# Turning the combine weights of an expert layer by DMA transposes instead of TensorE transposes

## The reference, cut to what matters

```
logits   = einsum('bsd,etd->bset', xn, se)          # 4 batches, 2048 rows, 8 x 128 slots
dispatch = softmax(logits, axis=1)                  # over the rows
slots    = einsum('bsd,bset->betd', xn, dispatch)
h        = gelu(slots @ w1);  processed = h @ w2
combine  = softmax(logits.reshape(b, s, e * t), axis=-1)
out      = x + einsum('bnd,bsn->bsd', processed, combine)
```

## Time and profile before

| what | us |
|---|---|
| median of 3 runs | 1343.07 (1338.6 to 1345.66) |
| the profiled execution, its own time | 1331.78 |
| span of the profiled execution | 1329.8 |
| PE busy | 1187.9 (89%) |
| DVE busy | 924.9 (70%) |
| ACT busy | 745.6 (56%) |
| POOL busy, all of it in `attention` and its set-up | 242.3 (18%) |
| mean granted clock of TensorE, as a share of full speed | 0.946 |

### The profile page before, as it was taken

One profiled execution on the slowest core, in us unless ns is written; L12 is line 12 of the kernel. 1 busy time (PEld: TensorE's weight loads), 2 busy tenths in 40 slices (PEclk: granted clock), 3 DMA queues, 4 the chain that ended last, 5 costly groups with the idle time before them and its releaser, 6 DMA issues.

```text
span 1329.8 us, 27115 instructions
## 1 busy us (share of the span) xinstructions
PE 1187.9 (89%) x8600; PEld 910.9 (68%) x8600; DVE 924.9 (70%) x2130; ACT 745.6 (56%) x1382; POOL 242.3 (18%) x275
## 2 busy tenths in 40 slices
PE   4498888989899885499999999999999999999999
PEld 2377777777777775248779548689558689467688
DVE  4688888887878863399545699445798445898444
ACT  3345565555555424258665558565468665577654
POOL 3555445554444431000000000000000000000000
PEclk8799999888988868699999999999999999999999
DMA  5122222323222121402112103212011212000012
GB/s 170 34 66 77 69 64 76 88 69 87 64 64 64 49 57 60 119 20 64 51 31 75 37 0 64 62 31 79 21 30 35 72 36 74 18 0 1 1 48 71
DMA packets 121979, 73.10 MB, mean 55 GB/s; under 512 B 49984, under 2 KB 119616, under 8 KB 121920
## 3 DMA queue, kind: packets, MB, share of 16 engines
q1 hardware_dynamic: 113200, 64.40, 17.2%
q10 hardware_dynamic: 8656, 7.87, 2.0%
q0 software_dynamic: 64, 0.00, 0.0%
HBM read 38.16 MB, written 25.69 MB: 48 GB/s over the span
## 4 chain that ended last, share of the span: by engine, by line
PE 39%; DVE 9%; issue 7%; ACT 2%; DVEq 1%; ACTq 0%; POOL 0%; POOLq 0%
PE m_wide L1792 13%; PE m_wide L1683 7%; PE m_wide L1770 6%; PE m_wide L1756 6%; PE m_wide L1781 4%; DVE m_Dm L1414 3%; ACT m_Eh L1571 2%; DVE m_cmax L1399 2%; DVE m_rmax L1401 2%; PE m_wide L1730 2%; DVE m_El L1422 1%; PE m_wide L1740 1%; DVE m_mcol L1407 0%; DVE m_sl L1436 0%; ACT m_L L1552 0%
## 5 line engine op out<-in xcount | busy, mean ns | idle before, releaser
L1683 PE MATMUL m_wide<-seT,XT 128*128 128x512 f16 x768 | 169.8, 382 | 30.5 <-ACTq L1543 25.5
L1730 PE MATMUL m_wide<-m_X,m_Eh 128*128 (+1 forms) x1024 | 172.6, 274 | 16.4 <-DVE m_El L1422 16.4
L1683 PEld LDWEIGHTS m_wide<-seT,XT 128*128 (+1 forms) x768 | 75.3, 98 | 121.1 <-ACTq L1543 25.9
L1792 PE MATMUL m_wide<-m_Ph,m_Th 128*128 128x257 f16 x512 | 140.4, 274 | 1.7 <-DVE m_Pl L1453 1.7
L1730 PE MATMUL m_wide<-m_X,m_El 128*128 128x257 f16 (+1 forms) x512 | 139.7, 273 | 0.0
L1792 PE MATMUL m_wide<-m_Ph,m_Tl 128*128 128x257 f16 x512 | 139.4, 272 | 0.0
L1792 PE MATMUL m_wide<-m_Pl,m_Th 128*128 128x257 f16 x512 | 139.1, 272 | 0.0
L1515 DVE TENSOR_TENSOR m_Tl<-m_wide,m_Th 128x1024 f16<-128x1024 f32 x64 | 78.4, 1224 | 68.2 <-ACT m_Th L1610 67.6
L1730 PEld LDWEIGHTS m_wide<-m_X,m_Eh 128*128 128x128 f16 x1024 | 97.7, 98 | 40.3 <-DVE m_El L1422 21.4
L1610 ACT CAST m_Th<-m_wide 128x1024 f16<-128x1024 f32 x64 | 64.7, 1011 | 86.3 <-PE m_wide L1781 86.3
L1564 ACT ACTIVATE m_E<-m_Dm,m_eshift 128x512 f32<-128x512 f32 x128 | 92.0, 722 | 32.0 <-DVE m_Dm L1414 30.7
(11 more groups left out here) (186 smaller groups left out, 2677.0 us busy)
## 6 DMA issues: line engine op xcount, KB each, us to landing
Mrep<-M_dram SPq DMA_DIRECT2D x16, 512.0 KB
x_dram<-x SPq DMA_DIRECT2D x16, 512.0 KB, 2.9
m_X<-X_dram SPq DMA_DIRECT2D x128, 64.0 KB, 1.8
m_x1t<-x_dram SPq DMA_DIRECT2D x64, 128.0 KB, 2.1
out_dram<-m_o SPq DMA_DIRECT2D x64, 128.0 KB, 1.7
x_<-in_L_attn_x_dram ACTq DMA_DIRECT2D x14, 512.0 KB, 4.0
X_dram<-Xh SPq DMA_DIRECT2D x16, 256.0 KB, 2.3
X_dram<-Xl SPq DMA_DIRECT2D x16, 256.0 KB, 5.8
```

The lines of the kernel that those rows point to most:

```text
L1683: last = pe.matmul(lg[t % 4], XT[:, sx * KD + k, bass.ds((4 * g + t) * P, P)], seT[:, ss, k, z * HS:(z + 1) * HS], start=(c == 0), stop=(c ...
L1730: last = pe.matmul(acc[v][q], e[t % 4][:, qs], X[:, sx, bass.ds(4 * g + t, 1), 0:XW].rearrange("q a n -> q (a n)"), start=first and e is E ...
L1792: last = pe.matmul(co[p], a[p][:, es], pp[:, e, 0:XW], start=(c == 0), stop=(c == 3 * NS - 1))
```

## The change

Both halves of the weights are made before they are turned. ACT takes the exponent in place in `L`, waits for it, and copies it to f16 (`Wh`); DVE subtracts (`Wl = L - Wh`). SP turns both by `dma_start_transpose` from SBUF into `Th` and `Tl`, which now have four buffers each and no longer come through PSUM. `Wh` and `Wl` have four buffers too, laid over `Eh`, `El` and `E`: tiles 0 and 1 over `Eh` and `El`, tiles 2 and 3 over `E`. Since `dispatch` reads `Eh` and `El`, ACT waits for both `B_ps` (the last dispatch matmuls) ahead of `weights(0, 0)`; since `hidden` keeps its f32 values in `E`, it waits for `hl_ok` ahead of `weights(0, 2)`. The transposes on TensorE and the tile `Ec` are gone. The loads of `x1t` and the stores of `o` leave SP; POOL issues them, in the same order.

```diff
-                def turn(h, p):
-
-                    n = b * HB + h + 1
-                    pe.wait_ge(Ec_ok[p], n)
-                    pe.wait_ge(Tl_ok[p], n)
-                    for e in range(NS):
-                        last = pe.transpose(tp[p][:, e * P:(e + 1) * P], Ec[p][:, e * P:(e + 1) * P], ident[:, :])
-                    last.then_inc(tp_ps[p], 1)
...
+            def turn(b, k, t):
...
+                sp.wait_ge(co_ps[t % 2], n)
+                sp.sem_inc(turning, 1)
+                sp.wait_ge(Wh_ok[t], m)
+                sp.sem_inc(turning, 1)
+                sp.dma_start_transpose(Th[t][:, :, :], Wh[t]).then_inc(T_in[t], 16)
+                sp.wait_ge(Wl_ok[t], m)
+                sp.sem_inc(turning, 1)
+                sp.dma_start_transpose(Tl[t][:, :, :], Wl[t]).then_inc(T_in[t], 16)
...
+            with pool.Fori(0, B) as b:
+                with pool.Fori(0, HB) as h:
+                    n = pool.snap(b * HB + h + 1)
+                    for p in range(2):
+                        pool.wait_ge(o_ok[p], n)
+                        pool.sem_inc(going, 1)
+                        pool.dma_start(x1t[p][:, :], x1_dram[bass.ds(b, 1), bass.ds(h * 2 * P + p * P, P), :]
+                                       .rearrange("b q d -> (b q) d")).then_inc(x1_in[p], 16)
+                    for p in range(2):
+                        pool.wait_ge(o_ok[p], n + 1)
+                        pool.sem_inc(going, 1)
+                        pool.dma_start(out[bass.ds(b, 1), bass.ds(h * 2 * P + p * P, P), :]
+                                       .rearrange("b q d -> (b q) d"), o[p][:, :]).then_inc(o_out[p], 16)
...
-                    dve.tensor_tensor(Tl[p][:, :], tp[p][:, :], Th[p][:, :], ALU.subtract).then_inc(Tl_ok[p], 1)
...
+                    dve.tensor_tensor(Wl[t], L[:, bass.ds(4 * k + t, 1), :].rearrange("q a n -> q (a n)"), Wh[t],
+                                      ALU.subtract).then_inc(Wl_ok[t], 1)
...
+                    row = L[:, bass.ds(4 * k + t, 1), :].rearrange("q a n -> q (a n)")
+                    act.activation(row, row, ACT.Exp, bias=nrm[:, bass.ds(4 * k + t, 1)]).then_inc(Ec_ok[t], 1)
+                    free = act.snap(act.to_reg(32 * m))
+                    act.wait_ge(pc, 1)
+                    act.wait_ge(Ec_ok[t], m)
+                    act.wait_ge(T_in[t], free)
+                    act.copy(Wh[t], row).then_inc(Wh_ok[t], 1)
...
                 act.wait_ge(A_dve, nb)
+                for p in range(2):
+                    act.wait_ge(B_ps[p], (2 * b + 2) * HB + 2)
                 weights(0, 0)
                 hidden_high(0)
...
+                processed_high(1, range(0, 2))
+                for p in range(2):
+                    act.wait_ge(hl_ok[p], (2 * b + 2) * (NF // 2) + 2)
+                weights(0, 2)
+                processed_high(1, range(2, QS))
+                weights(0, 3)
...
+                def combine(k, t):
+                    p, n = t % 2, b * HB + 2 * k + t // 2 + 1
+                    pe.wait_ge(T_in[t], 32 * (b * QB + k + 2))
                     pe.wait_ge(o_ok[p], n)
```

More of the change, by code:

```diff
@@ L1291, in moe @@
         Pl = sb("Pl", [P, NS, XS], F16)
-        Ec = two("Ec", [P, E_SLOTS])
-        Th = two("Th", [P, E_SLOTS], F16)
-        Tl = two("Tl", [P, E_SLOTS], F16)
+        Th = [sb(f"Th{u}", [P, NS, P], F16) for u in range(4)]
+        Tl = [sb(f"Tl{u}", [P, NS, P], F16) for u in range(4)]
         cden = two("cden", [P, 1])
@@ L1327, in _ @@
         def _(sp):
-            for p in range(2):
-                sp.sem_inc(o_out[p], 16)
+            for u in range(4):
+                sp.sem_inc(T_in[u], 32)
             def load_XT(b):
@@ L1343, in load_X, with turns @@
                                      .rearrange("b q d -> (b q) d")).then_inc(X_in, 16)
[L1345 to L1355, removed]
+            def turn(b, k, t):
+                m = sp.snap(sp.to_reg(b * QB + k + 1))
+                n = sp.snap(sp.to_reg(b * HB + 2 * k + t // 2 + 1))
+                sp.wait_ge(pc, 1)
+                sp.wait_ge(co_ps[t % 2], n)
[6 more added lines that the diff above has]
+                sp.dma_start_transpose(Tl[t][:, :, :], Wl[t]).then_inc(T_in[t], 16)
+            def turns(b):
+                with sp.Fori(0, QB) as k:
+                    for t in range(4):
+                        turn(b, k, t)
             sp.sem_inc(XT_in, 32)
@@ L1448, in hidden_low, with processed_low @@
                             .then_inc(hl_ok[f % 2], 1)
-                def processed_low(v):
-                    for q in range(QS):
+                def processed_low(v, qs):
+                    for q in qs:
                         dve.wait_ge(Ph_ok[q % 2], (2 * b + v) * (QS // 2) + q // 2 + 1)
@@ L1526, in finish @@
                                              ALU.mult, ALU.add).then_inc(o_ok[p], 1)
+                slots_low(0)
+                slots_out(1, range(QS))
                 low_weights(0, 0)
-                processed_low(1)
+                hidden_low(0)
+                slots_low(1)
+                processed_low(0, range(QS))
+                hidden_low(1)
                 low_weights(0, 1)
[L1531 to L1536, removed]
+                processed_low(1, range(0, 2))
+                low_weights(0, 2)
+                processed_low(1, range(2, QS))
+                low_weights(0, 3)
+                with dve.Fori(0, QB - 1) as k:
+                    for t in range(4):
+                        finish(k, t)
+                        low_weights(k + 1, t)
+                for t in range(4):
+                    finish(QB - 1, t)
         @block.scalar
@@ L1831, in _ @@
                     pe.wait_ge(Pl_ok[p], cut_to)
-                with pe.Fori(0, HB - 1) as h:
-                    for p in range(2):
-                        combine(h, p)
-                        turn(h + 1, p)
-                for p in range(2):
-                    combine(HB - 1, p)
+                with pe.Fori(0, QB) as k:
+                    for t in range(4):
+                        combine(k, t)
 def build(nc, io, out):
```

87 lines of the change are left out of this document (37 added, 50 removed).

## The result

The changed kernel takes 1374.64 us (median of 4 runs, 1366.12 to 1381.67), beside 1340.84 us for the kernel before (4 runs, 1336.38 to 1345.66). The ratio is 1.0249 with a 95% interval of 1.0178 to 1.0320: it is slower by 2.5%. All ratios here are taken from fast executions alone, since now and then an execution of any kernel is 1 to 2% longer at a lower granted clock (two of the four of e3 are, its profiled one among them). The profiled execution took 1373.25 us, with a span of 1371.7.

A forecast was written before the change was run, and what follows sets the result against it. TensorE was taken to bound the kernel before, the residual loop on POOL the changed one. Four batches at -1.5 us are -6, the end adds +2: 1343 - 4 = 1339 us, with a range of 1312 to 1385.

The forecast's parts named there:

- c: Residual loop in the combine stage: time from one odd finish's end to the next's, forecast 6.95 us for two tiles.
- GpSimd instead of SyncE: Residual loop: two longer issues on POOL add 0.4 to 0.8 us, taken as 0.6; no extra landing time.
- the transposes in the way: Residual loop: a 256 KB transpose ahead holds the DMA engines 0 to 0.9 us; half, 0.45, was taken.
- The end of the stage: End of each batch's combine stage: last two combines need 3.2 us after the loops, ending at 741.9 us in batch 0.
- The lead-in: Ahead of the combine stage: PE waits 1.7 us a batch in hidden(0); with processed(1), the stage starts 2.35 us later.
- SP's loop: SP issuing two transposes a tile in the combine stage: 3.2 us a tile, ending at 738.2, ahead of 741.9.
- T: SP's time to issue one 128 x 1024 transpose: taken as 1.3 us, deciding the pace from 1.45 on.
- SP as the pace: Rival, combine stage: transposes take 1.70 us to issue, a tile 4.0 us; 1363 us in all, chance 0.17.
- Dear source: Rival, combine stage: transposes out of SBUF cost more than out of DRAM; at 2.5 us each 1443 us, chance 0.09.
- DVE holding POOL: Rival, residual loop: low_weights on DVE holds up POOL's store issue for 1.29 us; c 8.24, 1370 us, chance 0.07.
- POOL as quick as SP: Rival, residual loop: POOL no slower than SP; c 5.9, -7.8 us a batch, 1313 us, chance 0.17.
- The four tiles: Rival, combine stage: a tile's way through four buffers, some 7.4 us, keeps tiles from getting ahead; given nothing.

The follow-up runs named there:

- e3: Changed kernel with only the high half of the weights turned by DMA and used again in place of the low half: ratio 1.0208 to the kernel before.
- e2: Changed kernel with GpSimd issuing each next residual load ahead of the store: 1340.72 us, ratio 1.0052 to the kernel before.
- e5: Changed kernel without any DMA transposes in the combine stage, which reads constant weights: 1337.4 us, ratio 0.9997 to the kernel before.
- e4: Changed kernel with tile 0's copy moved behind hidden(0), only its exp staying ahead: 1367.39 us, ratio 1.0284 to the kernel before.
- e1: Kernel before with residual loads and result stores issued by GpSimd, transposes still on TensorE: 1334.87 us, ratio 1.0021.
- e7: Changed kernel with the load ahead of the store, plus one spare 128 KB load a tile from GpSimd: 1372.62 us, ratio 1.0243 to the kernel before.
- e9: Changed kernel with load ahead of store and tile 0's copy later, odd tiles turned on TensorE again: 1308.81 us, ratio 0.9833 to the kernel before.
- e8: Changed kernel with load ahead of store and tile 0's copy and low half behind hidden(0): 1330.25 us, ratio 0.9965 to the kernel before.
- e6: Changed kernel with load ahead of store and only the high half turned, used again for the low: 1309.61 us, ratio 0.9766 to the kernel before.

## Why the prediction was wrong, point by point

**What bounds the stage: right.** The residual loop replaced TensorE as the pace, as forecast; the waits, the pairs of gaps and the place are those named. e2 shows it by removal. The range given for this very case, 1323 to 1354 (c of 6.3 to 7.6), does not hold the time; the wide one, 1312 to 1385, does only by its rivals.

**The term that failed: c, forecast 6.95 us, measured 8.21**, and with it the sign, since break-even stood at 7.2. By its parts:

| part of c | forecast | measured | from |
|---|---|---|---|
| loop before, with its rest | 5.9 | 5.56 | rest 2.21, not 2.55 |
| GpSimd instead of SyncE | +0.6 | +0.92 | e5 |
| the transposes in the way | +0.45 | +1.73 | changed kernel against e5 |
| sum | 6.95 | 8.21 | |

The third row is the miss: it is 1.28 us off, and the two others, 0.34 too high and 0.32 too low, cancel by luck. The working bounded it by 0 to 0.9 us, the bytes of one transpose at the full rate, and took half. That assumed one transpose in front of the load, at random, and a load that is served at once behind it. In the trace nothing is random: SP's transposes of a pair wait for the `low_weights` behind the even finish, which the load before has released; they come out one behind the other, one mostly 0.8 us ahead of the load and the next mostly 0.5 to 0.8 behind it, in every round but a batch's last. And the price is not that of the bytes. In 22 of these 24 rounds the load lands within 0.25 us of the transpose issued just ahead of it, 3.8 to 4.5 us after its own issue, as if it were served together with the whole of it; why, no run shows. e3, with one transpose issued 0.65 us ahead of the load, still costs 1.38 us (3.75 - 2.37), over the bound. Even at the bound c would have been 7.4 and the time, by the prediction's own sum, 1350: the sign, but not the size.

The second row was a third too low, and priced the wrong thing. The longer issue (0.54 us against 0.36) does not count: store to load is 1.20 us on POOL and 1.27 on SP. What counts is GpSimd's reaction to the semaphore, 0.70 us where SP took 0.03 (702.75 to 702.78), and a landing that is 0.32 later (X 2.37 against 702.75 + 3.35 - 704.05 = 2.05). The prediction took the extra landing as 0 from two tiny transfers at the start of the kernel. The first-byte times of the Trainium skill (DMA: Bandwidth & Descriptors, Specifications) put a transfer from GpSimd 0.4 us behind one from SyncE, an estimate from the page's two figures; the 0.32 us measured here are near it. The Trainium skill (DMA: Bandwidth & Descriptors, Anatomy of one DMA) fits a transfer from GpSimd as 2.0 us and the bytes at 436 GB/s, an estimate of 2.30 us for 128 KB; without transposes beside it the load takes 2.37.

**The end of the stage: undersized.** The prediction let the last two combines end 3.2 us after an odd finish, and the last finish 0.7 later. They start with the even finish before it, so 4.8 us, and then TensorE ran at half clock (below): the last c is 7.33 us. That is 3.4 us in batch 0 that no step of the prediction had.

**The lead-in: right.** 1.7 us a batch in `hidden(0)` was forecast and measured (6.9 / 4), and goes with e4. Between stages 2.35 were forecast in all; 3.2 came. **After the last finish:** +2 forecast, +2.6 measured.

**SP's loop: right, its neighbour not.** T was forecast at 1.3 us; an undisturbed issue takes 1.25, and SBUF as a source made the issue no dearer. A tile was forecast to take SP 3.2 us; by itself it needs 3.07 (e2). But the DMA engines were priced at 2.5 us a tile, "hidden, but full", from 291 GB/s in a 1 MB transpose. The queue's share grew from 13.4% of 1334.2 us (e1, no weights turned) to 26.4% of 1371.7, which is 183 us for 128 transposes, 1.43 us of share each; with 0.47 for each plain transfer (4.5% of 1371.7 over 130) a tile asks for 3.8. At the 1.04 to 1.19 that the load-first stage holds this is an estimate of 3.2 to 3.7 us, over TensorE's 2.65. The prediction counted bytes where the engines' time a transfer is dearer. So even with a perfect residual loop the stage would have stopped near 49 us (e2), at 13.3 to 14.5 us of SP for four tiles, and the ceiling of 55.7 us was out of reach: by SP's own 12.3, with the DMA engines' stretching on top.

**The rivals.** SP as the pace: not in the changed kernel; behind it, yes (e2), with the DMA engines on top (e7). Dear source: not in the issue. DVE holding POOL: no, each issue takes 0.54 us, and the 0.70 of reaction is the same in e1, where DVE stands idle in that moment (from 702.47 to 703.70); that it gave c = 8.24 and 1370, near what came, is luck. POOL as quick as SP: no, by 0.92 us. The four tiles: no, of TensorE's 56.1 us of waiting ahead of `combine` 49.8 are for `finish`. Of the 0.45 that the prediction gave to slower, 0.12 stood for the cause that came. What led the central value astray was a cost halved because it was thought random, and priced by its bytes.

## What to carry to other kernels

Before a transfer's wait is priced, look at what releases its neighbours: two queues that hang on the same chain of events collide in every round, and the collision is to be counted whole, by when the transfer in front lands and not by its bytes. A load whose buffer is free belongs ahead of the store that it waits behind, which here brought the ratio from 1.0249 to 1.0052. When one engine is relieved by moving its work to another resource, price that resource and the queue that feeds it by their own time per operation, and move only as much as evens the two out: with the load ahead of the store and the copy later, every second tile won 1.7% (e9) and all of them 0.35% (e8).

## What was not expected of the hardware

*The clock fell after TensorE's longer waits.* Windows of one us in the changed kernel, in the stage and at its end (PE busy and granted clock are the second and the seventh figure):

```profile
712.00:713.00 1.00, 0.00 (x0) 0.00 (x0) 0.00 (x0) 0.78 (x1) 0.00 (x0) 1.00 1.19 127
715.00:716.00 1.00, 1.00 (x6) 0.68 (x5) 0.96 (x3) 0.43 (x1) 0.54 (x1) 0.50 1.10 231
...
746.00:747.00 1.00, 0.00 (x0) 0.00 (x0) 0.19 (x1) 0.00 (x0) 0.00 (x0) 1.00 1.10 266
749.00:750.00 1.00, 1.00 (x6) 0.72 (x5) 0.00 (x0) 0.00 (x0) 0.36 (x2) 0.50 0.63 225
```

TensorE stood from 711.7 to 714.7 and from 744.8 to 747.35; after each the granted clock fell from 1.00 to 0.50 (2.4 to 1.2 GHz), back at 1.00 by 718 and 752, and a window of one us shows 6 or 7 matmuls instead of 11 or 12. A third wait, from 728.5 to 731.2, had the same effect. In mid-stage, where `combine` has slack before the next residual, it adds little to c; at its end the two last combines took some 7.1 us (747.35 to 754.5) instead of 5.3. In e9, with no gaps, the windows of the stage show 1.00 throughout.

*GpSimd pauses once.* In the last batch of e1, e3, e4, e5 and the changed kernel the fourth round is 1.1 to 3.4 us longer than its neighbours: c of 9.10 in e1, 11.33 in the changed kernel. In e1 the odd finish ends at 1300.45 and its store goes out at 1303.84, 3.4 us later instead of 0.70, with a gap that nothing in the profile explains:

```profile
1298.76 0.55 POOL L1380 DMA_DIRECT2D out_dram<-m_o  x1 [2.13 <-DVE m_o L1530]
1303.84 0.54 POOL L1380 DMA_DIRECT2D out_dram<-m_o  x1 [4.53 <-issue]
```

It stands ahead of POOL's 116th transfer in all five; in e2, e6, e8 and e9 the same transfer, there a store, comes 2.80 us behind the load before it, where 0.1 is usual. No run asked for the cause, which stays open.
